# A residual chain with conditioned weights: transposed output with its factor at the eviction, unrolled loops, stores from ScalarE

## What is computed

```python
ae = layernorm(cond, ln_g, ln_b)                        # cond: (8, 512)
xw = gelu(ae @ w1 + b1) @ w2 + b2                       # w2: 512 x 8192
x_a, x_b = split(xw), each reshaped to (b, 512, RANK)   # RANK = 8
layer = base_layer + einsum('bdr,bkr->bdk', x_a, x_b)
x = x + (x + x @ layer)
ys = cond / sqrt(512)
d = rsqrt((ys*ys) @ (weight*weight) + 1e-8)             # (8, 512)
x = x + ((x * ys) @ weight) * d
```

## Time and profile before

| | |
|---|---|
| median of 3 runs | 321.53 us (321.42 to 321.64) |
| span of the profiled execution | 319.6 us; no other time of that execution is given |
| PE, DVE, ACT, POOL busy | 307.4, 157.8, 135.8, 43.2 us |
| mean granted TensorE clock | 0.989 |
| moved by DMA | 56.7 MB, 177 GB/s |

### The profile page before, as it was taken

One profiled execution on the slowest core, in us unless ns is written; L12 is line 12 of the kernel. 1 busy time (PEld: TensorE's weight loads), 2 busy tenths in 40 slices (PEclk: granted clock), 3 DMA queues, 4 the chain that ended last, 5 costly groups with the idle time before them and its releaser, 6 DMA issues.

```text
span 319.6 us, 4287 instructions
## 1 busy us (share of the span) xinstructions
PE 307.4 (96%) x1425; PEld 234.9 (74%) x1425; DVE 157.8 (49%) x230; ACT 135.8 (42%) x219; POOL 43.2 (14%) x59
## 2 busy tenths in 40 slices
PE   7979999999999958999999999999999999999995
PEld 7756555555566835888888888888888888888884
DVE  4898626262658896544255236146235434443300
ACT  3465233232366323546436337426435444454321
POOL 5545000000004991101001001001010000000000
PEclk9999999999999996999999999999999999999999
DMA  6921888788860130034375355437436545643342
GB/s 192 384 91 49 277 297 267 289 269 299 332 222 17 57 107 2 1 120 156 122 262 193 137 197 205 189 131 257 179 105 246 198 147 180 249 155 124 131 164 98
DMA packets 12892, 56.72 MB, mean 177 GB/s; under 512 B 2016, under 2 KB 2048, under 8 KB 8656
## 3 DMA queue, kind: packets, MB, share of 16 engines
q1 hardware_dynamic: 12880, 56.57, 49.4%
HBM read 39.77 MB, written 16.79 MB: 177 GB/s over the span
## 4 chain that ended last, share of the span: by engine, by line
PE 85%; DVE 7%; ACT 4%; issue 2%; DMA 1%; SPq 0%; DVEq 0%; ACTq 0%
PE tile L913 54%; PE tile L834 20%; PE acc L814 5%; PE aux L852 2%; DVE rtmp L601 1%; PE tile L770 1%; DMA base<-in_w0T 1%; DVE xs L615 1%; DVE base L521 1%; DVE rtmp L605 1%; ACT xs L351 1%; DVE xs L529 1%; DVE xs L526 1%; ACT rs L379 1%; PE aux L876 1%
## 5 line engine op out<-in xcount | busy, mean ns | idle before, releaser
L834 PE MATMUL tile<-rs,w0s 128*128 128x512 f32 x336 | 85.3, 406 | 5.3 <-ACT base L384 5.3
L913 PE MATMUL tile<-pev,xs 128*128 128x512 f32 x384 | 90.3, 389 | 0.0
L913 PE MATMUL tile<-w0s,xs 128*128 128x512 f32 x384 | 89.6, 389 | 0.0
L834 PEld LDWEIGHTS tile<-rs,w0s 128*128 128x128 f32 x336 | 63.0, 193 | 32.9 <-issue 14.4
L913 PEld LDWEIGHTS tile<-pev,xs 128*128 128x128 f32 x384 | 72.1, 188 | 15.0
L913 PEld LDWEIGHTS tile<-w0s,xs 128*128 128x128 f32 x384 | 72.1, 188 | 15.0
L456 ACT COPY stream<-tile 128x512 f32<-128x512 f32 x64 | 37.6, 587 | 99.9 <-PE tile L913 98.9
L615 DVE TENSOR_TENSOR xs<-xr,xs 128x1024 fp32r<-128x1024 f32 x32 | 40.5, 1267 | 62.5 <-ACT xs L414 62.5
L379 ACT CAST rs<-rtmp 128x512 fp32r<-128x512 f32 x28 | 17.4, 622 | 56.5 <-DVE rtmp L605 56.5
L697 DVE TENSOR_TENSOR base<-aux,base 128x512 f32 (+1 forms) x32 | 21.2, 686 | 34.7 <-PE aux L852 34.7
L414 ACT CAST xs<-xr 128x1024 fp32r<-128x1024 f32 x32 | 33.5, 1051 | 0.0
(11 more groups left out here) (112 smaller groups left out, 143.8 us busy)
## 6 DMA issues: line engine op xcount, KB each, us to landing
stream<-in_w2u SPq DMA_DIRECT2D x16, 1024.0 KB, 4.9
xr<-in_xT SPq DMA_DIRECT2D x32, 512.0 KB, 3.4
out<-stream SPq DMA_DIRECT2D x15, 1024.0 KB, 4.1
dbs<-d_kept SPq DMA_DIRECT2D x6, 256.0 KB, 4.5
base<-in_w0T SPq DMA_DIRECT2D x4, 256.0 KB, 4.7
w1s<-in_w1n SPq DMA_DIRECT2D x4, 256.0 KB, 5.0
base<-in_wm SPq DMA_DIRECT2D x1, 1024.0 KB, 7.2
stream<-in_w0n SPq DMA_DIRECT2D x1, 1024.0 KB, 6.6
```

Of the source, the lines that this page charges most:

```text
L834: last = nc.tensor.matmul(tiles[cc][:], w0s[:, u, kc, cols], rs[:, kc, v], start=kc == 0 and (u, v) == (0, 0), stop=kc == KC - 1 and (u, v ...
L913: mm = nc.tensor.matmul(tiles[tt][:], xs[:, h, u, cc, toks], p_split(parity)[:, v, cc], start=n == 0, stop=n == 11)
```

## The change

1. The main product is turned over: P is stationary and x moves, so a tile is 128 output columns by 512 tokens. A factor per output column is then a factor per partition, and the d of each batch is applied by ScalarE's eviction (`scale=dts[...]`). P is built without d: the right side of the middle product is weight diag(ys) + diag(1/d), where 1/d is `dinv`. `d_kept`, its loads, `dbs`, `dbc` and the d in C go; four small matmuls on `dib` bring 1/d to C. The host turns the output back.
2. `first_tiles` and GpSimd's repair of batch 0 go. Batch 0's middle product is made by `base_tiles` like the others, after d. There are 29 warm-up matmuls instead of 11. w1 is loaded ahead of w0, and ScalarE squares it.
3. The middle products of batches 0 to 4 (`STORED`) stand ahead of the main products and are kept in `base`. Those of batches 5 to 7 are made by `late_base` into the `aux` banks between the two halves of batches 4 to 6, and are split from PSUM. The split of P has two buffers of its own, `qs`.
4. The 16 w2 units stand in batches 0 to 2, by the table `W2_AFTER`: up to two after a group.
5. All loops are written out.
6. Stores are of 512 KB, a pair of tiles, with four places, and ScalarE issues them on its own DMA queue behind the second eviction of the pair.

```diff
-LOOPED = 4
+STORED = 5
+W2_AFTER = {(0, 1): 1, (0, 2): 1, (0, 3): 1, (1, 0): 1, (1, 1): 1, (1, 2): 2, (1, 3): 2,
+            (2, 0): 2, (2, 1): 2, (2, 2): 2, (2, 3): 1}
...
             for kc in range(KC):
+                sp.dma_start(w1s[:, kc], w1n[:, kc]).then_inc(w1_loaded[kc], 16)
+            for kc in range(KC):
                 sp.dma_start(w0raw[:, kc], w0T[:, kc]).then_inc(w0_loaded[kc], 16)
-                sp.dma_start(w1s[:, kc], w1n[:, kc]).then_inc(w1_loaded[kc], 16)
...
+            def evacuate_out(b, h, o):
+                n = main_tile(b, h, o)
+                m = (b * HALVES + h) * 2 + o // 2
+                act.wait_ge(tile_done, n + 1)
+                if o % 2 == 0 and m >= 4:
+                    act.wait_ge(stored[m % 4], 16 * (m // 4))
+                nc.scalar.activation(pairs[:, m % 4, o % 2], tiles[n % BANKS][:], ACT.Copy,
+                                     scale=dts[:, b, o:o + 1]).then_inc(bank_free, 1)
+                if o % 2 == 1:
+                    act.wait_ge(bank_free, n + 1)
+                    nc.scalar.dma_start(out[b, h, o // 2], pairs[:, m % 4]).then_inc(stored[m % 4], 16)
...
+                if late:
+                    for cp in range(2):
+                        evacuate_out(b, 0, cp)
+                        r_high(b + 1, 2 * cp)
+                        r_high(b + 1, 2 * cp + 1)
+                for o in (2, 3):
+                    evacuate_out(b, 0, o)
+                if late:
+                    for cc in range(KC):
+                        q_high(b + 1, cc)
...
+                nc.vector.tensor_scalar(slot, w1s[:, kc], ys[:, b, kc:kc + 1], None, ALU.mult).then_inc(r_scaled, 1)
+                dve.wait_ge(r_scaled, n + 1)
+                blk = slot[:, kc * P:(kc + 1) * P]
+                nc.vector.scalar_tensor_tensor(blk, ident[:], dinv[:, b, kc:kc + 1], blk, ALU.mult,
+                                               ALU.add).then_inc(r_eyed, 1)
...
+            add_two(1)
+            r_scale(0, 0)
+            add_two(2)
+            r_scale(0, 1)
+            r_low(0, 0)
             add_two(3)
+            r_scale(0, 2)
+            r_low(0, 1)
             dve.wait_ge(prm_loaded, 48)
...
+            def late_base(b):
+                pe.wait_ge(r_lo, b * KC + KC)
+                for cc in range(KC):
+                    aux_free(b, cc)
+                    cols = slice(cc * P, (cc + 1) * P)
+                    for kc in range(KC):
+                        for u, v in ((0, 0), (0, 1), (1, 0)):
+                            last = nc.tensor.matmul(aux[cc % 2][:], w0s[:, u, kc, cols], rs[:, kc, v],
+                                                    start=kc == 0 and (u, v) == (0, 0), stop=False)
+                    if cc == KC - 1:
+                        last.then_inc(r_used, 3)
+                    rank_tile(b, cc, start=False)
...
+            for b in range(B):
                 pe.wait_ge(p_lo, b * KC + KC)
                 for h in range(HALVES):
...
+                        for cc in range(KC):
                             for u, v in ((0, 0), (0, 1), (1, 0)):
+                                last = nc.tensor.matmul(tiles[n % BANKS][:], qs[:, b % 2, u, cc, cols],
+                                                        xs[:, h, v, cc], start=cc == 0 and (u, v) == (0, 0),
+                                                        stop=cc == KC - 1 and (u, v) == (1, 0))
+                        last.then_inc(tile_done, 1)
...
+                    if h == 0 and STORED <= b + 1 < B:
+                        late_base(b + 1)
```

More of the change, by code:

```diff
@@ L191, in _, with load_w2 @@
         def _(sp):
[L192 to L197, removed]
+            def load_w2(unit):
+                if unit >= 2:
+                    sp.wait_ge(acc2_steps, 1 + unit - 1)
+                sp.dma_start(stream[:, unit % 2], w2u[unit]).then_inc(w2_loaded[unit % 2], 16)
@@ L258, in _ @@
[L258 to L264 removed]
+            for unit in range(UNITS):
+                load_w2(unit)
+            for cp in range(2):
+                load_x(0, 0, cp)
@@ L375, in _ @@
[L375 to L384 removed]
+            r_high(0, 2)
@@ L813, in w2_unit, with base_tiles @@
                 for g in range(4):
-                    last = nc.tensor.matmul(acc2[32 * g:32 * g + 32, :], hz[:, j], stream[:, j % 2, g, :],
+                    last = nc.tensor.matmul(acc2[32 * g:32 * g + 32, :], hz[:, u // 4, u % 4], stream[:, u % 2, g, :],
                                             start=False, stop=True, skip_group_check=True)
                 last.then_inc(acc2_steps, 1)
-            def base_tiles(b, units=False, between=None):
+            def base_tiles(b, between):
@@ L855, in permute, with with_w2 @@
             def permute(bank, which, rows):
                 nc.tensor.matmul(bank[:], perm[:, which], rows, start=True, stop=True).then_inc(perm_done, 1)
-            with pe.Fori(1, LOOPED + 1) as b:
-                base_tiles(b, units=True)
+            def with_w2(b, kc):
+                if (b, kc) == (0, 0):
+                    pe.wait_ge(wm_loaded, 16)
+                    pe.wait_ge(ae_ready, 1)
+                    narrow(1, ae, wms).then_inc(h_done, 1)
+                    pe.wait_ge(b2_loaded, 16)
+                    pe.wait_ge(consts_ready, 4)
+                    nc.tensor.matmul(acc2[:], sel2[:], b2s, start=True, stop=True,
+                                     skip_group_check=True).then_inc(acc2_steps, 1)
+                    pe.wait_ge(h_copied, 1)
+                    nc.tensor.transpose(aux[0][:, 2 * P:3 * P], h_rows, ident[:]).then_inc(h_turned, 1)
+                for _ in range(W2_AFTER.get((b, kc), 0)):
+                    w2_unit()
@@ L861, in columns_and_c @@
+            for b in range(3):
+                base_tiles(b, with_w2)
             def columns_and_c(b, kc):
@@ L911, in main_step @@
                         for cc in range(KC):
                             for u, v in ((0, 0), (0, 1), (1, 0)):
-                                mm = nc.tensor.matmul(tiles[tt][:], xs[:, h, u, cc, toks],
-                                                      p_split(parity)[:, v, cc], start=n == 0, stop=n == 11)
-                                n += 1
-                        mm.then_inc(tile_done, 1)
-                        if h == 0 and not last:
-                            rank_tile(b + 1, 1 - parity, tt, group)
```

714 lines of the change are left out of this document (280 added, 434 removed).

## The result

The changed kernel takes 328.46 us (median of four runs, 327.33 to 330.56) against 321.58 us before on the same chip: a ratio of 1.021, 95% interval 1.018 to 1.025, so 2.1% slower. The forecast was 324.8 us, inside a range of 320.5 to 330: the sign and the mechanism held, but the loss is 6.9 us instead of 3.3. The profiled execution took 327.92 us with a span of 325.9.

What follows compares the result with a forecast made beforehand. The kernel was taken to be bound by PE's work plus the waits ahead of 135.6 us. Stages of 33.8 + 42.8 + 28.9 + 213.1 + 4.3 gave 322.9; with 1.9 from profiled span to median, 324.8, range 320.5 to 330.

Steps and rivals of the forecast that it cites:

- Start: Start and batch 0: 33.8 us; d chain from 9.9, `ae` at 19.5, 2.4 for four VectorE operations meeting GpSimd's.
- The w2 waits: Batches 1 and 2, 42.8 us: PE waits from unit 6 on, 1.1 to 1.5 us a pair, 6.2 in all.
- the rule: w2 queue: a load lands 4.9 us after issue, and two transfers queued behind each other are 2.5 apart.
- the upper bound: Batches 1 and 2: w2 waits of 8.5 us in all if a load takes 5.3 to land.
- The slower stream's rival: w2 stage: 3.0 us a unit and a landing of 5.4 give waits of 8.9, total 327.5; 4 in 100.
- The clock: Rival: the clock falls in w2 waits of 1.5 us, six groups at half rate cost 17.7, total 342; 3 in 100.
- Third stage: Batches 3 and 4, columns and C: 28.9 us, from 26.8 of work, 1.4 late at the end, 0.7 for masks.
- Main products: 213.1 us: 180.5 as before plus 32.65 for the middle products of batches 5 to 7, with no wait.
- The rival of a new wait: Main products: ScalarE's copies over 1.2 us late make each late product wait some 2, total 330.8; 8 in 100.
- Factor and stores: Main products: 0.12 us more per scaled eviction, 8 us of ScalarE; 0.45 per store, 14 us; no PE wait.
- the cover that the prediction named: Main products: 1.2 us of slack before a late middle product, and 4 us for the high parts behind the stores.
- Tail: After the last main product: 4.3 us, with 0.1 more for the factor and 3.1 for the 512 KB store.

Runs made afterwards that it cites:

- the copy: The changed kernel run again unchanged on chip A, beside the kernel before: 333.22 us, ratio 1.031.
- four slots: The changed kernel with four buffers for w2 loads instead of two, on chip A: 321.85 us, ratio 0.997.
- the eight matmuls: The changed kernel with eight small matmuls on constants before the h product, on chip C: 327.61 us; with four w2 buffers as well, 318.36 us.
- the best version: The changed kernel with four w2 buffers and `ae` computed behind VectorE's first low part instead of the second, on chip C: 315.77 us, ratio 0.982.

## Why the prediction came out as it did

**Start.** The order of the steps was right: first middle group, PE idle, `ae`; but `ae` came 1.2 late. The chain of waits (start us, us, what) shows where:

```profile
8.19 0.65 PE aux L599 x8
...
9.52 1.15 PE tile L592 x4
10.68 0.23 PE aux L617
10.93 0.20 DVE lns L475
...
14.11 1.43 DVE rtmp L443
15.56 1.25 DVE rtmp L446
```

Its matmuls ran slower than those of the copy (x8 0.65 against 0.43, x4 1.15 against 0.64), so the d chain starts at 10.93 instead of the 9.9 of the sum (9.94 in the copy's timeline). Behind it all came as summed, in other parts: beside L226 on GpSimd a scale took 1.43 instead of 0.41, a diagonal 1.25 instead of 0.35 and the first step of `ae` 1.18 instead of 0.2, 2.9 us for three meetings where the sum has 2.4 for four; against that the undisturbed operations are each somewhat shorter than taken.

**The w2 waits.** This is the step that failed. Batches 1 and 2 were put at 42.8 and took 45.8: every load was taken to land 4.9 us after its issue, or 2.5 behind the one ahead, and a wait was priced at its length alone. Measured were waits of 7.3 for 6.2, 1.4 of lost clock where the sum has nothing, and 0.5 of slower units. The mechanism held (a slot's round of 6.0 against a pair of 4.95), and four slots take the whole away. The 2.5 held too, as a rate. In the copy two loads issued 2.1 and 2.5 us behind another landed 2.5 after it, and with four slots and `ae` moved, where the queue is not empty for 14 us, it moves 417 GB/s (the last figure), 2.5 us a unit:

```profile
46.00:60.00 14.00, 14.00 (x83) 7.38 (x82) 5.25 (x11) 3.62 (x7) 0.00 (x0) 1.00 1.01 417
```

What the sum had wrong is that no load is late. The one issued at 48.87 landed at 54.96, 3.4 behind the one ahead, and the one issued at 63.08 landed 3.0 behind: 0.9 and 0.5 more than the rule. With 4.8 for the other landings the steps of the prediction give 5.9, and with these 1.4 the 7.3. In the copy one load took 7.3 us, 2.5 too long, and the waits are 9.6. The trace of before has late loads as well, 6.0 and 6.1 us, both issued 3.8 us or more behind another; there a slot came round each 7.9, so nobody waited, and the sum took the median, 4.9. With two slots and pairs PE pays each of them. What makes a load late no run shows. (Stepped again, a landing of 5.3 gives waits of 7.4, not the 8.5 of the upper bound.)

The slower stream's rival (4 in 100, waits of 8.9) comes near this size by another way, for its rate is not what the queue has: the stage's 294 GB/s at a share of 0.82, 359 GB/s of busy time, is a mean over loads with pauses between them. The Trainium skill, DMA: Bandwidth & Descriptors, section Bandwidth, gives about 358 GB/s as what HBM grants one core. The 417 GB/s over 14 us does not agree with that, and the measurement decides.

**The clock.** It was a rival at 3 in 100 and 342 us, because I read the earlier trace rows as a threshold: 3.9 us of idle did it, 0.9 did not. In the profiled execution after, a wait of 2.3 us in a stretch with others did it, for about 1.4 us of loss; in the copy 2.1 us behind 0.6 and 0.7 did it, for 4.3, and 3.5 did it, for 1.5. It is no threshold between these either: a wait of 2.5 us in the copy left the clock at 1.00. The mechanism was a part of the forecast's own case and not a case beside it: some of it belonged into the sum. How the profiles divide: of the eight with 2.1 us of idle time before the h product seven have a clock of 0.50 to 0.79 between 18 and 30 us, and the four in which it is filled or gone have 1.00. All four ran on chip C, where no kernel with that idle time ran, so a part of the chip is not ruled out for the start; but on C too the clock fell, behind the w2 waits. What it costs shows best in one kernel on one chip: four slots took 319.5 and 319.9 us at a mean clock of 0.994 and 0.995, and 322.2 to 323.3 at 0.983. That the eight matmuls compute nothing, and the start then holds its clock, speaks for PE's idle time itself as the cause, whatever PE waits for.

**Third stage.** 27.8 against 28.9. Neither 1.4 for the end nor 0.7 for the masks came in full; PE waits 0.8 us once, before the main products, on VectorE's low parts of q (L561).

**Main products.** 213.7 against 213.1, and 213.4 to 213.7 in every profile, so only 0.6 of the 6.9 us is here. The rival of a new wait did not come; at a late product PE waits 0.2 us at most. Factor and stores, priced at 8 and 14 us of ScalarE, cost 0.3 each, which together are the 0.6; the rest is under the cover that the prediction named. That the unrolled loops cost nothing rests on this figure and on rows without gaps; no run undid the unrolling.

**Tail.** 3.8 against 4.3: the 512 KB land in 2.9.

**What stays open.** Why the clock fell in the start of the copy and not in the first measurement's profile (one of that measurement's four runs, 330.56 us at 0.982, looks like the copy's). The profiles differ in how fast the sixteen warm-up matmuls ran (5.20 us, without a gap behind them, against 3.74), but on chip B they took 3.97 with no gap before the first group, 0.73 us of idle time within it, and the clock fell all the same. What makes single loads late is open too. Nor was the kernel before given a filled gap before its own main products (four slots could give it nothing, since PE has no gap in its w2 stage), so how much of the best version's gain needs the change is not known.

## What to carry to other kernels

Two units behind a group instead of one can turn a stream that was never late into the bound: compare the round of a buffer (use, issue, landing) with the work between its two uses, in the tightest place of the order and not on average, leave room there for a load that lands up to 2.5 us late, and add a slot before blaming the rate. Price idle time of TensorE at more than its length, since the next microseconds may run at half clock; moving its producer forward was worth 2.6 us more here than filling it with matmuls that compute nothing. Here four slots and three small operations moved turned a change that was 2 to 3% slower into one 1.8% faster than before.

## What was not expected of the hardware

- Halving a load from 1 MB took 1.1 us off its landing when it was alone (4.8 to 3.7), and only some 0.3 off the distance to the one ahead when it was issued 0.9 us behind it (2.5 to 2.2).
- Loads of 1 MB on one queue, issued 3.9 us or more behind one another, mostly land in 4.7 to 5.0 us, but some take 1 us or more beyond that (6.0 and 6.1 in the kernel before, 5.9 in the copy). A queue kept full moved 417 GB/s for 14 us all the same.
- One program, unchanged, had medians of 328.5 and 333.2 us in two measurements in which the kernel before had 321.6 and 322.2. Of the 6.1 us between the two profiles some 3.7 are gone by the first w2 unit, with the granted clock at 0.64 and 0.51 in 12 us of the start, and 2.4 in the w2 stage, mostly one late load.
- A VectorE operation on a 128x32 tile takes 1.18 us beside a GpSimd operation, about as much extra as a 128x512 one (0.41 to 1.43): in these meetings the cost did not go with the size of VectorE's operation.
